# A graph network's adjacency: one-hot outer products on TensorE in place of GpSimd scatters

## The reference

```python
h = relu(layernorm(x))
for w1, b1, w2, b2 in three_gin_layers:             # widths 64, 128, 64
    agg = segment_sum(h[src] * edge_weight, dst) + h
    h = relu(agg @ w1 + b1) @ w2 + b2               # relu between the layers
x = x + h
h = relu(layernorm(x))
x = x + attention_network(h, edges, node_vec)       # three graph attention layers, 8 heads,
                                                    # batch norm, a sine embedding of node_vec
```

## Time and profile before

| what | value |
|---|---|
| median of 3 runs | 5954.8 us (5954.24 to 5956.43) |
| the profiled execution: its time, its span | 5958.3 us, 5956.3 us |
| TensorE busy in it, its mean granted clock | 2547.3 us (43%), 0.666 |
| VectorE, ScalarE, GpSimd busy | 2667.4, 508.0, 3822.0 us |
| scatters into adj_t | 876, 1068.9 us busy |
| gathers of the attention layers | 2664, 2517.7 us busy |

### The profile page before, as it was taken

The page is one execution under the profiler, slowest core; times in us unless marked ns, Lnnn a source line. Parts: engine busy times, 40 slices in busy tenths (PEclk is TensorE's granted clock), DMA queues, the critical chain, the costliest instruction groups (busy, mean ns, idle before and its releaser), DMA issues. The chain is left out here.

```text
span 5956.3 us, 52364 instructions
## 1 busy us (share of the span) xinstructions
PE 2547.3 (43%) x7810; PEld 1679.5 (28%) x7810; DVE 2667.4 (45%) x7267; ACT 508.0 (9%) x1859; POOL 3822.0 (64%) x3789
## 2 busy tenths in 40 slices
PE   0000000000069985656566665655555644444443
PEld 0000000000023333434344444433343433333333
DVE  5534454455640004555555535555555333333333
ACT  2200000000000012000000030000000300000001
POOL 1477787788810015777777737777777377777774
PEclk9855555555588887777777687777777755555555
DMA  7200000000055543444444515444444232222222
GB/s 271 67 3 3 4 3 4 4 3 4 5 210 233 232 163 77 111 109 109 109 109 109 104 53 109 109 109 109 109 109 109 36 57 56 56 57 56 56 56 28
DMA packets 338667, 493.49 MB, mean 83 GB/s; under 512 B 248114, under 2 KB 249911, under 8 KB 325626
## 3 DMA queue, kind: packets, MB, share of 16 engines
q0 software_dynamic: 150096, 317.52, 22.9%
q1 hardware_dynamic: 172715, 131.66, 7.0%
q10 hardware_dynamic: 15824, 43.96, 1.9%
HBM read 438.14 MB, written 55.12 MB: 83 GB/s over the span
## 5 line engine op out<-in xcount | busy, mean ns | idle before, releaser
L465 POOL DMA_INDIRECT rows_all<-gat_tab,ell x2664 | 2517.7, 945 | 821.3 <-issue 627.3
L920 PE MATMUL banks<-rows_all,ident 128*128 128x264 f32 (+1 forms) x5328 | 1803.7, 508 | 1557.0 <-PEq L107 1557.0
L920 PEld LDWEIGHTS banks<-rows_all,ident 128*128 128x128 f32 x5328 | 1303.6, 285 | 2056.3 <-issue 1869.0
L469 POOL DMA_INDIRECT adj_t<-post_w,post_i x876 | 1068.9, 1220 | 298.2 <-issue 293.3
L814 PE MATMUL banks<-x_t,h_st 128*64 128x512 f32 (+1 forms) x532 | 211.0, 554 | 1455.0 <-PEq L107 1455.0
L1384 DVE COPY lrel<-m_all 128x8 f32 x666 | 137.7, 207 | 1525.3 <-DMA rows_all<-gat_tab,ell 1203.8
L1409 DVE TENSOR_TENSOR rows_all<-rows_all,banks 128x1024 f32<-128x1024 f32 (+1 forms) x666 | 685.0, 1042 | 136.4 <-DVE ex_in L1397 136.4
L814 PEld LDWEIGHTS banks<-x_t,h_st 128*64 128x64 f32 x532 | 72.1, 139 | 1591.4 <-issue 1591.4
L741 ACT ACTIVATE banks<-ex_in 128x40 f32<-128x40 f32 x666 | 138.3, 208 | 3076.8 <-ACTq L107 3076.8
L465 POOL DMA_INDIRECT x_res<-x_d,node_i x26 | 24.5, 943 | 543.8 <-DMA x_d<-x_res 536.2
L1362 DVE TENSOR_TENSOR acc<-acc,banks 128x264 f32 (+1 forms) x675 | 259.5, 384 | 45.2 <-DVEq L107 12.4
(11 more groups left out here) (254 smaller groups left out, 2172.3 us busy)
## 6 DMA issues: line engine op xcount, KB each, us to landing
x_t<-adj_t SPq DMA_DIRECT2D x18, 3200.0 KB, 10.4
y_t<-adj_t SPq DMA_DIRECT2D x18, 3200.0 KB, 10.4
rows_all<-gat_tab,ell POOLq DMA_INDIRECT x2664
adj_t<-rows_all ACTq DMA_DIRECT2D x25, 1600.0 KB, 23.5
adj_t<-post_w,post_i POOLq DMA_INDIRECT x876, 2.1
ell<-ell_d SPq DMA_DIRECT2D x666, 2.5 KB
x_t<-adj_t SPq DMA_DIRECT2D x2, 1600.0 KB, 6.5
x_t<-key_d SPq DMA_DIRECT2D x1, 1664.0 KB, 6.4
```

What stands on the lines that cost most here:

```text
L465: return g.indirect_dma_start(out=dst, out_offset=None, in_=table, in_offset=bass.IndirectOffsetOnAxis(ap=idx, axis=0))
L469: return g.indirect_dma_start(out=table, out_offset=bass.IndirectOffsetOnAxis(ap=idx, axis=0), in_=data, in_offset=None)
L920: last = t.matmul(sum_ps[u % SUMS][:, 0:width], ident[:, :], rows[u][:, r * width:(r + 1) * width], start=(r == 0), stop=(r == SLOTS - 1))
```

## The change

Node n no longer stands in tile n / 128, partition n % 128, but in partition n / 26, column n % 26, and x is loaded so. A tile is now one column, 128 nodes, and the adjacency is built one pair of destination tiles at a time, 13 pairs. For each of 128 partitions d of a pair, its two nodes' edge slots (2 x 64 = 128) lie on the 128 partitions after a transpose. Two one-hot rows per slot, of the source's partition (128 wide, hi_hot) and of its column (52 wide: 26 for each of the two nodes, times the weight, lo_hot), are made by VectorE; TensorE multiplies the one with the other and so adds up all slots, repeats included; ScalarE copies the product from PSUM into adj (x_t or y_t) in SBUF. While the next pair is built, TensorE uses the pair just made for the first GIN layer, and SyncE stores it to adj_d for the other two, which read it back pair by pair. The two pairs last used stay in their buffers.

The zero fills, the scatters, the shifts and the comparisons are gone. Ranks, records, plan and lists, which need no adjacency, move behind the first layer: the ranks and the records into the second layer's loop on VectorE and ScalarE, the lists of the 26 tiles into the third layer's loop (LISTED_AT), stored by GpSimd instead of SyncE, into ell_d with the partition outermost. The sine's steps go there too. The first layernorm moves ahead of rp. The weight loads on ScalarE's queue start right after the first counts. The code for nodes with over 64 edges (more) is there but guarded.

```diff
+            def one_hot(u, c):
+                n = c % PART_RING
+                take(dve, hot_free[n])
+                for q in range(GROUP_DST):
+                    d = c * GROUP_DST + q
+                    v.tensor_scalar(hi_hot[n][:, q, :], lane[:, :], src_hi[u][:, d:d + 1], None, ALU.is_equal)
+                    last = v.tensor_scalar(lo_hot[n][:, q, :], lane[:, 0:PAIR * T], src_lo[u][:, d:d + 1], src_w[u][:, d:d + 1], ALU.is_equal, ALU.mult)
+                last.then_inc(hot_ready[n], 1)
...
+            def part(c, made):                      # TensorE
+                n = c % PART_RING
+                take(pe, hot_ready[n])
+                take(pe, part_free[n])
+                for q in range(GROUP_DST):
+                    last = t.matmul(part_ps[n][:, q, :], hi_hot[n][:, q, :], lo_hot[n][:, q, :], start=True, stop=True)
+                last.then_inc(made, 1)
...
+            def keep_part(u, c):                    # ScalarE
+                n = c % PART_RING
+                take(act, part_made[n])
+                act.sem_inc(hot_free[n], 1)
+                s.activation(adj_cells[u][:, :, :, c * GROUP_DST:(c + 1) * GROUP_DST], part_cells[n], ACT.Copy).then_inc(part_free[n], 1)
...
+            def build_pair(u, first=False):         # TensorE; c == 2, 3, 4, 5 of GROUPS = 8
+                for c in range(GROUPS):
+                    if c == TURN_AT:
+                        turn_edges(1 - u)
+                    if not first:
+                        if c == AGG_AT:
+                            pe.sem_inc(adj_made, 1)
+                            take(pe, own_ready)
+                            aggregate(h_own, h_in, 1 - u, 1 - u, 0, T)
+                        if c == MID_AT:
+                            gin_hidden(0)
+                        if c == OUT_AT:
+                            gin_out(0)
+                    part(c, part_made[c % PART_RING])
...
+            for l in (1, 2):                        # TensorE, second and third layer
+                h = h_mid if l == 1 else h_in
+                take(pe, h_ready)
+                for i, k in enumerate(PAIR_ORDER[l]):
+                    u = PAIR_HOME[l][i]
+                    if i >= 2:
+                        take(pe, adj_landed[u], 16)
+                    own = h[:, k * PAIR:(k + 1) * PAIR, :]
+                    aggregate(own, h, u, i % 2, 0, T // 2)
                     if i:
-                        gin_out(i - 1, STRIP)
+                        gin_hidden(l)
+                    aggregate(own, h, u, i % 2, T // 2, T)
+                    if i:
+                        gin_out(l)
...
+            for i, k in enumerate(PAIR_ORDER[2]):   # VectorE, third layer
+                take(dve, B_made[0])
...
+                signal(B_free[0])
+                link(v.tensor_tensor(x_at, x_at, at, ALU.add))
+                if i == PAIRS - 1:
+                    signal(x1_ready)
+                if i == 2:
+                    plan_tiles()
+                for t in LISTED_AT.get(i, ()):
+                    list_tile(t)
+                if i >= 8 and i < PAIRS - 1:
+                    next(sin, None)
```

More of the change, by code:

```diff
@@ L231, in program @@
         rows = [rows_all[:, u * SLOTS * max(gat_row):(u + 1) * SLOTS * max(gat_row)] for u in range(RING)]
[L232 to L238, removed]
+        zero_row, junk_a = rows_all[0:1, 0:NP + 1 + P], rows_all[:, 0:NP]
@@ L555, in _ @@
-            chunks = pool.value_load(meta[0:1, 1:2], min_val=0, max_val=CHUNKS)
-            pool.wait_ge(scattered, chunks * GROUP + SCATTERED)
-            pool.sem_inc(adj_built, 1)
+                    take(pool, ell_ready)
+                    row = nc.s_assert_within(start + s * PER_BLOCK, 0, CHUNKS - PER_BLOCK,
+                                             skip_runtime_bounds_check_because="CHUNKS has room for every tile's last block")
+                    g.dma_start(ell_d[:, bass.ds(row, PER_BLOCK), :], ell_new[:, :, :]).then_inc(ell_stored, 16)
@@ new lines, in gin_hidden, with gin_out @@
+            def gin_hidden(l):
+                take(pe, agg_copied)
+                take(pe, B_free[0])
+                t.matmul(gin_mid_ps[0:GIN_MID[l], :], w1[l][:, :], agg_sb[:, :], start=True, stop=True).then_inc(mid_made[0], 1)
+            def gin_out(l):
+                take(pe, mid_copied[0])
+                for j in range(PAIR):
+                    last = t.matmul(gin_out_ps[:, j, :], gin_mid[0:GIN_MID[l], j * P:(j + 1) * P], w2[l][:, :], start=True, stop=True)
+                last.then_inc(B_made[0], 1)
@@ new lines, in _ @@
+            turn_edges(0)
+            take(pe, more_known["pe"])
+            more = pe.value_load(more_i[0:1, 0:1], min_val=0, max_val=BLOCKS)
+            build_pair(0, first=True)
+            take(pe, h_ready)
+            pe.wait_ge(weights_landed, 16 * WEIGHTS)
+            with pe.Fori(0, PAIRS // 2):
+                for u in (1, 0):
+                    build_pair(u)
+            for n in range(PART_RING):
+                take(pe, part_free[n])
+            pe.sem_inc(adj_made, 1)
+            take(pe, own_ready)
@@ L874, in _ @@
+            emb_out(i)
+            for u in range(2):
+                take(pe, B_free[u])
+                pe.sem_inc(B_free[u], 1)
             take(pe, h_ready)
```

826 lines of the change are left out of this document (449 added, 377 removed).

## The result

The changed kernel takes 5279.45 us (median of 4 runs, 5270.5 to 5284.93) where the kernel before took 5955.43 on the same chip: a ratio of 0.8864, 95% interval 0.8848 to 0.8879, 676 us less. The prediction was 5236, its range 5050 to 5350, its likeliest case alone 5180 to 5290: the result lies near the upper end of that case. The profiled execution took 5278.14 us with a span of 5276.6.

What follows compares the result with a forecast made beforehand. GpSimd's 876 scatters bound a 1410 us stage. Build to 1086 us, second layer to 1253, third 217 to 1470, then 51: first reduction at 1521, 718 earlier, so 5240 profiled, 5236 median; range 5050 to 5350.

Steps and rivals of the forecast that it cites:

- likeliest case: Whole kernel: TensorE's products at the lower clock set the build, VectorE as taken; 5180 to 5290 us, chance 0.58.
- Start of the build: Before the adjacency build: gathers, rp1, then some 9 us of steps; the build starts at 113 us.
- The product at 0.44 us: Build, TensorE: a float32 outer product takes two 0.22 us records at clock 0.50; 7.04 us a group, 56.3 a pair.
- the rival with the risen clock: Build: TensorE granted 2.4 GHz, product 0.22 us, VectorE sets the pace, 63 us a pair, 5100 in all; chance 0.20.
- my 0.35 to 0.41: Build, VectorE: two one-hot rows per destination cost 0.35 to 0.41 us, taken as 0.385, 6.2 us a group.
- the estimate by its formula: Build, VectorE: 58 cycles plus half the columns gives 0.215 us for the two one-hot instructions of a destination.
- my 2.2 us for a pair's start: Build: at a pair's start VectorE's loop, pick and own rows run 2.2 us over, part of 3.6 us stalls.
- the stalls at 43 us in all: Build: TensorE's waits for VectorE, 3.6 us a pair, 43 in all, which one-hots at 0.215 us would take out.
- Second layer: Second graph layer: 13 pairs of 11.5 + 0.4 + 0.4 us, taken as 164 us, with 3 for the tail.
- a list costs 5.8 us, so this layer follows VectorE: Third layer: 23 lists at 5.8 us each on VectorE outlast TensorE's 12.4 us a pair; 217 us in all.
- My 166 us for hidden lists: Third layer: lower bound of 166 us if the lists' work were hidden, against 217 forecast.
- Behind it: After the third layer: last three lists 17 us, 26 gathers 33 us and landing; 51 us to the first reduction.

Runs made afterwards that it cites:

- run 1: Changed kernel with each outer product given 104 moving columns in place of 52: 5925.52 us, 0.8890 of the kernel before on its chip.
- run 2: Changed kernel with three wide VectorE instructions per group in place of 32: 5934.38 us, 0.8903 of the kernel before on its chip.
- run 8: Changed kernel with the lists of all 26 tiles moved behind the third layer: 5353.0 us (one run).
- Run 3: Changed kernel with two list buffers, so GpSimd waits for a store's landing only before the next store: 5976.36 us, 0.8969 of the kernel before on its chip.
- run 10: Changed kernel with 104-column products, wide VectorE instructions, two list buffers, loop written out, aggregation in three parts: 5679.48 us, 0.8506 of the kernel before on its chip.
- run 6: Changed kernel with both 104-column products and three wide VectorE instructions per group: 5021.78 us, 0.8437 of the kernel before on its chip.

## Why the prediction was right, and where its terms were off

The mechanism was right: the scatters gave up their 1410 us, TensorE's products at the lower clock set the build, and the attention block stayed. The stages that I added up came out at 1562 for my 1521: 18 us less in the build, 8 more in the second layer, 41 in the third, 9 behind it, 40 in all (the parts are rounded). That the sum stays within the likeliest case owes something to luck, since 18 us the one way hide part of 58 the other way.

- **Start of the build.** 113 predicted, 113.6 measured; nothing ahead of it got in the way.
- **TensorE.** The product at 0.44 us held: 7.04 us a group. The clock stayed at 0.50 between aggregations, so the rival with the risen clock is out, for 52 columns. That columns don't set the pace is shown by run 1 (7.00 us with 104 columns). The rule that I weighed (the Trainium skill, TensorE: Matmul & The Clock Gate, Part 1, sustained matmul work releases the half rate) doesn't hold for these products as I read it: run 2 keeps TensorE busy without a gap at 0.50. With 104 columns in place of 52 the same stream rose to 1.00. Width is not all there is to it: in the stretch of the kernel before that I weighed, half of TensorE's busy time was in records of 512 columns, over 64 partitions, and it stayed at 0.50 too:

```profile
2017.14 1.97 PE L844 MATMUL banks<-w,rows_all 128*128 128x64 f32 x8
2019.04 2.07 PE L849 MATMUL banks<-rows_all,w 64*128 64x512 f32 x2
```

- **VectorE.** 0.415 us per destination (0.20 and 0.21 from start to start) against 0.385, 6.65 us a group against 6.2: just above my 0.35 to 0.41, under the 0.44 at which I would have been wrong, and below TensorE's 7.04, so it cost only in the stalls. (My 0.5 ns for a column was misread: 287 and 245 ns for 128 and 64 columns make 0.66.) The Trainium skill (VectorE: DVE Perf Modes, section on the TRN2 errata) was right in its advice, wide instructions, which run 2 shows at 4.3 us a group; the estimate by its formula, 0.215 us per destination, is half of what the rows show for narrow ones. The same section says that this formula is too low and that a fixed term of about 150 cycles was measured in place of 58; an estimate with 150, for the same two ops, is 0.41 us, close to the 0.415 of the rows. The rows:

```profile
587.74 0.30 DVE L1240 TENSOR_SCALAR rows_all<-lane,src_lo,src_w 128x52 f32<-128x52 f32 x1
587.96 0.28 DVE L1239 TENSOR_SCALAR rows_all<-lane,src_hi 128x128 f32<-128x128 f32 x1
588.15 0.30 DVE L1240 TENSOR_SCALAR rows_all<-lane,src_lo,src_w 128x52 f32<-128x52 f32 x1
```

- **Errors that cancelled in the pair** (72.6 us for 74, of which my terms add up to 73.3; rounding up alone put 8 us into the build). The two groups behind an aggregation saved 5.2 us of clock, not 3 (3.77 and 5.14 for twice 7.04), and the aggregation took 12.9 and 0.9, near my 13.7. TensorE waited 80.8 us for the one-hots in the build, some 6 a pair, not 3.6: my 2.2 us for a pair's start were too little where the long loop turns (4.95 us of VectorE). I had put the stalls at 43 us in all; run 2 took 49 us of waits out, and 72 us in all.
- **Second layer.** 26 records of 256 columns take 5.78 us, 0.222 each, where I took 0.21; with 52 a pair this is 0.5 to 0.6 us a pair and the 8 us.
- **Third layer: the mis-sized term.** The step is "a list costs 5.8 us, so this layer follows VectorE". That TensorE would wait at B_free behind the lists was right; the size was not. From the first list to the last output 191 us pass (1310.5 to 1501.5). The sine's steps take 18.8 of them (18 predicted), the nine outputs 7, and 7.3 are VectorE waiting for TensorE, which itself had waited for a load (run 8); the rest, 158 us, is 6.9 for each of the 23 lists, 1.1 more than 5.8 and 25 us in all. The other parts of the 41 are the 7.3, for which I had nothing, and 9 ahead of the first list: it starts behind the fourth output (LISTED_AT begins at i = 3), not behind the plan. What sets a list is not VectorE's work (4.7 us) but its waits for GpSimd's chain of gather, store, landing and loop turn (45.4 us for gathers, some 6 for the buffer, 2.2 a list together), which I had called "about as much" and not worked out. Run 8 prices the chain at 6.2 with the transfers idle; the rest comes where the adjacency's loads run beside it. Run 3, which takes only the landing off the chain, gives 25 us back. My 166 us for hidden lists was too low as well: without lists it is 190.5, 7.6 of that the wait for the held-up load. (And my 265 for 8 us a tile is 268 by its own terms.)
- **Behind it.** From x1 to the reduction 60.3 us, not 51: the last three lists take 22 us (17 predicted), and 4.8 pass from the last store to the first gather of x, for which I had nothing.
- **The attention block** did not change, and ScalarE's copies (864 ns per group) and the stores of adj_d stayed hidden, as said.

## What to carry to other kernels

When two engines hand each other small pieces, a gain on one is worth only what the other has left: here 72 and 78 us alone, 254 together, part of it by the clock (0.67 and 0.85 alone, 0.93 together). Price a chain over a queue (gather, store, landing, loop turn, next gather) as a chain, link by link, before calling it "about as much" as another engine's work. And where TensorE's records last the same whatever their columns, wider products that cost nothing can still gain by the clock: read the granted clock beside the length of a record, before and after.

## What the runs showed of the hardware

- TensorE at 0.50 although busy without a gap (2 us in the changed kernel, 4 us in run 2), with 52 float32 columns a record; at 1.00 within one group with 104 columns, whose records then take 0.117 us instead of 0.22. A wait of 1.9 us was followed by a slower group in run 10 (5.38 us for 3.75), one of 2.33 us in run 6 once by a slower group and once by none, and waits of 5 us by 5.58 and 7.00 us.
- A bfloat16 product of 128 x 128 weights and 52 columns takes 0.05 us at the clock at which the float32 one takes 0.44.
- Behind a VectorE instruction of 52 columns with two scalars per partition the next one starts no sooner than behind one of 128 columns with one: after 0.20 to 0.21 us either way. Over a whole group, 2048 columns take 2.29 us.
- The turn of a loop with a body of over 500 VectorE instructions leaves that engine idle for 4.9 us; in run 2, with a short body, the idle time is gone.
- A store of 13 KB in single cells (vec_d<-recs) takes 22.9 us to land, and a load of 3.3 MB issued meanwhile comes late (TensorE waits 6.7 to 7.6 us for it).
- Chips differ in the attention block. A gather there takes as long on all of them, but on some GpSimd stands nearly twice as long between them. First the changed kernel, then run 10 (busy us, mean ns, idle before):

```profile
L486 POOL DMA_INDIRECT rows_all<-gat_tab,ell x2664 | 2517.4, 945 | 822.3 <-issue 624.0 <-POOLq L117 198.0 <-PEq L994 0.3
```

```profile
L487 POOL DMA_INDIRECT rows_all<-gat_tab,ell x2664 | 2516.8, 945 | 1530.0 <-issue 789.7 <-POOLq L118 727.2 <-PEq L1009 13.1
```

The block lasts 3715 us in the one and 4431 in the other, and the second layer, which reads 3.4 MB per pair, 175 us and 193. What makes these chips slower there stays open.
